# Adding the causal mask on VectorE instead of TensorE, with the values' products moved ahead of the turning of the weights

## The reference

```python
def step(carry, qkv):
    M, z = carry
    q, k, v = qkv
    sq = _sigma(q)                                  # elu(q) + 1
    denom_q = jnp.sum(sq * z[:, :, None, :], axis=-1, keepdims=True) + EPS
    A_mem = jnp.matmul(sq, M) / denom_q
    scores = jnp.matmul(q, jnp.swapaxes(k, -2, -1)) * inv_sqrt_dk
    scores = jnp.where(causal, -jnp.inf, scores)    # above the diagonal of 64 x 64
    A_dot = jnp.matmul(jax.nn.softmax(scores, axis=-1), v)
    A_s = beta * A_mem + (1.0 - beta) * A_dot
    sk = _sigma(k)
    denom_k = jnp.sum(sk * z[:, :, None, :], axis=-1, keepdims=True) + EPS
    V_prev = jnp.matmul(sk, M) / denom_k
    M_new = M + jnp.einsum('bhtk,bhtv->bhkv', sk, v - V_prev)
    z_new = z + jnp.sum(sk, axis=-2)
    return ((M_new, z_new), A_s)
```

## Time and profile before

| what | us |
|---|---|
| median of 3 runs (lowest, highest) | 1970.64 (1970.03, 1977.45) |
| the profiled execution, its own time | 1964.26 |
| its span, first to last instruction | 1962.4 |
| attention stage in it | about 41 to 1268 |
| one pass with look-ahead / with choice | 38.38 / 38.52 |
| busy in the whole span: TensorE, VectorE, ScalarE | 1860.4, 1440.1, 873.7 |

### The profile page before, as it was taken

The page is one execution under the profiler, slowest core; times in us unless marked ns, Lnnn a source line. Parts: engine busy times, 40 slices in busy tenths (PEclk is TensorE's granted clock), DMA queues, the critical chain, the costliest instruction groups (busy, mean ns, idle before and its releaser), DMA issues. The chain is left out here.

```text
span 1962.4 us, 72363 instructions
## 1 busy us (share of the span) xinstructions
PE 1860.4 (95%) x32380; PEld 1575.6 (80%) x32380; DVE 1440.1 (73%) x3478; ACT 873.7 (45%) x1494; POOL 151.6 (8%) x179
## 2 busy tenths in 40 slices
PE   6999999999999999999999999769899999889998
PEld 5888888888888888888888888647776767667997
DVE  7888788888888777777777777566587887876222
ACT  4344344434344443443343434225587777764110
POOL 1000000000000000000000000141100000001000
PEclk9999999999999999999999999779999999999999
DMA  4112111211221121111111112046500000014000
GB/s 146 46 46 78 57 46 49 81 52 46 63 67 41 35 57 46 36 39 59 41 35 44 54 41 67 30 146 184 164 13 12 12 12 22 5 42 161 23 12 22
DMA packets 65668, 109.52 MB, mean 56 GB/s; under 512 B 4736, under 2 KB 25232, under 8 KB 65360
## 3 DMA queue, kind: packets, MB, share of 16 engines
q1 hardware_dynamic: 59584, 85.74, 13.9%
q0 software_dynamic: 5776, 19.15, 3.1%
HBM read 60.31 MB, written 27.26 MB: 45 GB/s over the span
## 5 line engine op out<-in xcount | busy, mean ns | idle before, releaser
L1021 PE MATMUL proj<-xnT_high,held 128*128 128x256 f32 x1536 | 233.8, 287 | 2.1 <-DVE xnT_low L749 2.1
L1021 PEld LDWEIGHTS proj<-xnT_high,held 128*128 128x128 f32 x1536 | 202.5, 190 | 7.8 <-DVE xnT_low L749 2.6
L425 POOL TENSOR_TENSOR As<-T 128x512 f32<-128x512 f32 x64 | 84.4, 1319 | 1173.0 <-DVE T L844 1173.0
L1021 PE MATMUL proj<-xnT_low,held 128*128 128x256 f32 x1024 | 162.9, 281 | 0.0
L2017 DVE CUSTOM_DVE_ANT_0 Sm<-Sp,held 128x1023 f32<-128x1023 f32 x128 | 155.5, 1216 | 9.7 <-DVE r L1278 3.0
L1915 ACT ACTIVATE Sm<-Sm,least 128x1023 f32<-128x1023 f32 x128 | 146.7, 1146 | 13.7 <-DVE least L2017 12.9
L1021 PEld LDWEIGHTS proj<-xnT_low,held 128*128 128x128 f32 x1024 | 139.3, 189 | 0.0
L2063 PE MATMUL Sp<-KS,held 128*128 128x512 f32 x256 | 95.0, 454 | 34.5 <-DVE least L2017 29.4
L484 ACT ACTIVATE Pq<-Pq 128x1024 f32<-128x1024 f32 x64 | 68.0, 1062 | 121.3 <-DVE Pq L813 120.9
L464 ACT ACTIVATE QT<-proj 128x512 f32<-128x512 f32 x64 | 38.0, 594 | 179.9 <-PE proj L1021 179.9
L1967 DVE COPY PTs<-Tp 128x512 f32<-128x512 f32 x128 | 88.1, 688 | 40.3 <-PE Tp L2075 39.9
(11 more groups left out here) (322 smaller groups left out, 4394.1 us busy)
## 6 DMA issues: line engine op xcount, KB each, us to landing
VS<-DV SPq DMA_DIRECT2D x64, 264.0 KB, 3.9
xin<-in_x SPq DMA_DIRECT2D x32, 512.0 KB, 4.9
out_rows<-xu SPq DMA_DIRECT2D x64, 256.0 KB, 2.0
mask_columns<-x1T SPq DMA_DIRECT2D x16, 512.0 KB, 5.4
xs<-in_w SPq DMA_DIRECT2D x16, 512.0 KB, 4.3
xe<-in_x SPq DMA_DIRECT2D x15, 512.0 KB, 3.6
QT<-in_wqT SPq DMA_DIRECT2D x1, 1024.0 KB, 6.2
KT<-in_wkT SPq DMA_DIRECT2D x1, 1024.0 KB, 9.3
```

The costliest lines, as they stand in the source:

```text
L425: pool.tensor_tensor(As[:, :], T1[:, :], T2[:, :], ALU.add).then_inc(s_as, 1)
L1021: ins = pe.matmul(bank[:, g * BT:g * BT + BT], w[hw][:, c, o:o + P], xnT[hx][:, c, :], start=n + c == 0, stop=n == 2 and c == G - 1)
```

## The change

TensorE's four mask products go away, and the scores are written with `start=True`; the wait for `s_t2` moves to the first score product. VectorE, in `row_max`, now first adds `causal` to the scores in four instructions (one for each of the four banks, 128 x 256 each), which read PSUM and write `Pq` in SBUF; the maximum and `less_max` then read `Pq`. On TensorE V0 stands in front of the turning 1, V1 in front of `pv` 1, and SK0, SK1 and XT0 all in front of `memory` 1. ScalarE copies V0 out before the turned weights. Nothing else moves, on any engine.

```diff
@@ ScalarE, half @@
                     feature(m, 1, "KT", KT, pn, 1.0, (s_sq, m * 2 + 4))
+                if stage1:
+                    v_tile(m, pn, 0)
                 p_turned(m, 1)
                 if stage1:
-                    v_tile(m, pn, 0)
                     v_tile(m, pn, 1)
@@ VectorE @@
             def row_max(m, a):
                 dve.wait_ge(s_S, m * 2 + (a + 1))
-                link(dve.tensor_reduce(mx[:, :, :], s_half(a), AX.X, ALU.max))
+                rows = Pq[:, :, :, :].rearrange("p g j k -> p j g k")
+                for j in range(J):
+                    ins = dve.tensor_tensor(rows[:, j, :, :], s_half(a)[:, j, :, :], bm(causal[:, :], G), ALU.add)
+                    if j < J - 1:
+                        done[0] += 1
+                        ins.then_inc(s_dve, 1)
+                link(ins)
+                link(dve.tensor_reduce(mx[:, :, :], rows, AX.X, ALU.max))
 
             def less_max(m, a):
-                dve.tensor_tensor(Pq[:, :, :, :].rearrange("p g j k -> p j g k"), s_half(a),
+                rows = Pq[:, :, :, :].rearrange("p g j k -> p j g k")
+                dve.tensor_tensor(rows, rows,
                                   mx[:, :, :].rearrange("p j (g o) -> p j g o", o=1).broadcast_to([P, J, G, SEG]),
                                   ALU.subtract).then_inc(s_sub, 1)
@@ TensorE @@
-            def mask(m, a):
-
-                pe.wait_ge(s_t2, m * 2 + a + 1)
-                for j in (0, 2, 1, 3):
-                    r = slice((j // 2) * SEG, (j // 2) * SEG + SEG)
-                    pe.matmul(S[:, j, a * 256:a * 256 + 256].rearrange("p (g k) -> p g k", g=G), identb[r, :],
-                              causal[r, :].rearrange("p (o k) -> p o k", o=1).broadcast_to([SEG, G, SEG]),
-                              start=True, stop=False, skip_group_check=True)
-
-            def scores(p, a, b):
+            def scores(m, p, a, b):
+                if b == 0:
+                    pe.wait_ge(s_t2, m * 2 + a + 1)
...
                         ins = pe.matmul(S[b * SEG:b * SEG + SEG, j, o:o + SEG], QT[q, p, g, t:t + SEG],
-                                        KT[q, p, g, t:t + SEG], start=False, stop=(g == G - 1),
-                                        skip_group_check=True)
+                                        KT[q, p, g, t:t + SEG], start=True, stop=True)
@@ TensorE, half @@
-                mask(m, 1)
-                scores(p, 1, 0)
-                scores(p, 1, 1)
+                scores(m, p, 1, 0)
+                scores(m, p, 1, 1)
                 a_and_b(m, p, 1)
                 as_transposes(m, m * 2, 0)
                 if stage1:
                     feature(m, "KT", wk, 1)
-                p_transposes(m, 1)
                 if stage1:
                     values(m, 0)
+                p_transposes(m, 1)
                 t_times_m(m, 2)
+                if stage1:
+                    values(m, 1)
                 pv(m, mh, p, 1)
                 if stage1:
-                    values(m, 1)
-                if stage1:
                     sk_rows(m, n2, 0)
-                memory(m, p, 1)
-                if stage1:
                     sk_rows(m, n2, 1)
                 if ln:
                     x_transposes(m, m + 2, p, "XT", 0)
+                memory(m, p, 1)
                 t_times_m(m, 3)
                 if stage1:
                     denominators(m, n, pn)
-                    mask(m + 1, 0)
-                    scores(pn, 0, 0)
-                    scores(pn, 0, 1)
+                    scores(m + 1, pn, 0, 0)
+                    scores(m + 1, pn, 0, 1)
                     den_transposes(m)
```

More of the change, by code:

```diff
@@ L1255, in _ @@
             x_transposes(None, 1, 1, "XT", 0)
-            mask(0, 0)
-            scores(0, 0, 0)
+            scores(0, 0, 0, 0)
             x_transposes(None, 1, 1, "XT", 1)
-            scores(0, 0, 1)
+            scores(0, 0, 0, 1)
             half(0, 0, 0, first=True)
```

## The result

The changed kernel takes 2108.89 us (median of 4 runs, 2103.41 to 2112.72); before took 1970.99 beside it. The ratio is 1.0686, with a 95% interval of 1.0667 to 1.0706: slower by 138 us. The profiled execution took 2108.63 us, its span 2106.9. The forecast was 2091 in a range of 2045 to 2115.

The account below looks back on a forecast made before the run. TensorE's products bound the kernel now; after the change, waits on VectorE would add 4.1 us to look-ahead passes (62) and 3.7 to choice passes (55), plus 3.5: +120 on 1970.6, so 2091. Own range 2070 to 2115, with rival 1 2045 to 2115.

Parts of the forecast that it names:

- The loop through VectorE: One pass, `a_and_b` 0 to the next, taking the later of TensorE and VectorE: 42.5 us with look-ahead, 42.2 with choice.
- the passes with choice: Passes without router rows, 15 to 29: 42.2 us each against 38.52, +3.7 a pass, 55 us in all.
- The clock: Rival 4: waits halve TensorE's clock from `a_and_b` 0 to `memory` 0; 2364, or 2182 in a third of passes; chance 0.07.
- a clock that leaves 1.00 in mid-stage: One of the signs named in advance that would show the forecast to be wrong.
- The additions: Four of 128 x 256 on VectorE before the maximum: 1.49 us a set, ends 1.13 and 1.73.
- V0's wait, XT0's and the scores' waits: TensorE waiting for `low_a`'s bank at V0 1.1 us, `xn` at XT0 1.4, `memory_part` 1 at scores 0 1.0.
- the time before `a_and_b` 0: TensorE waiting there 1.2 us for L799, `previous_values`, on VectorE.
- The saving of 0.64 us a pass: Two masks of 0.32 us taken off TensorE in each pass; 20.5 us for all 64.
- `start=True` at nothing: Overwriting scores costed at no gain; up to 0.4 us a pass was thought possible.
- Rival 2: TensorE's count decides and VectorE's 6.0 us idle takes the additions: 20.5 us saved, 1950; chance 0.08.
- Rival 3: Waits and savings cancel, within 0.5% (10 us); chance 0.03.
- Rival 1: Fewer waits, V0 does not wait: 1.1 us a pass or 33 us off, 2058; chance 0.12.

Follow-up runs that it names:

- adds_twice: The changed kernel with VectorE's four additions done twice, the second set writing the same values again; 2243.58 us, ratio 1.1381 to the kernel before.
- mask_only: The kernel before with the mask added on VectorE and scores with `start=True`, old TensorE and ScalarE orders kept; 2042.51 us, ratio 1.0360.
- tile_0: The kernel before with VectorE's additions for tile 0 alone, tile 1 keeping its mask products, old order; 2001.06 us, ratio 1.0173.
- tile_1: The kernel before with VectorE's additions for tile 1 alone, tile 0 keeping its mask products, old order; 2002.16 us, ratio 1.0174.
- v0_only: Against mask_only, V0 moved in front of the turning 1 on TensorE and ScalarE; 2047.55 us, ratio 1.0413 to the kernel before.
- low_a_mid: The changed kernel with `low_a` of AST0 between the additions and the maximum of tile 1; 2080.50 us, ratio 1.0564 to the kernel before.
- v1_back: The changed kernel with V1 behind `pv` 1 again, V0 still in front of the turning; 2108.11 us, ratio 1.0702 to the kernel before.

## Why the prediction was right

**The loop through VectorE: right.** Step by step, a look-ahead pass in the rows above against my sum:

| step | forecast, us | measured, us |
|---|---|---|
| `a_and_b` 0 to `memory` 0 | 9.09 | 529.32 - 520.24 = 9.08 |
| to `memory_part` 0, to the additions | 1.00 + 4.75 | 1.00 + 4.75 |
| additions | 1.49 | 1.44 |
| to the end of `low_a` AST0 | 2.39 + 0.68 | 3.08 |
| hand-over, V0 to `pv` 1 | 0.1 + 7.14 | 0.06 + 7.25 |
| `pv` 1 to `softmax_part` 1 | 1.21 | 548.11 - 546.90 = 1.21 |
| to `memory_part` 1 and its end | 5.45 | 510.50 - 505.03 = 5.47 |
| from there to `denominators` | 0.1 + 1.0 + 0.48 = 1.58 | 512.61 - 510.50 = 2.11 |
| to the end of `previous_values` | 6.04 + 1.49 | 518.81 + 1.28 - 512.61 = 7.48 |
| hand-over | 0.1 | 0.15 |

The forecast was 42.5, the pass takes 43.07. With choice 42.2 was forecast and 42.15 measured, and there too step by step: from `a_and_b` 0 at 953.06 it is 19.39 us to V0, 7.24 to `pv` 1, 1.20 to `softmax_part` 1, 5.15 to the end of `memory_part` 1 behind XT0 and `memory` 1, 1.53 to `denominators`, which there does wait for TensorE, and 7.64 to the next `a_and_b` 0.

**Where the 18 us between 2091 and 2109 are.** First, 0.53 us in each look-ahead pass, 8 us in all. This is the one step at which I took the wrong side as the later one: I had TensorE's way over the scores 0 and `den_transposes`, 1.58 us, but VectorE's own queue from the end of `memory_part` 1 to `denominators` takes 2.11. The passes have 43.07 us whether their scores 0 take 0.99 us from start to start (at 122.59), 1.15 as here, or 1.33 (at 165.65). The queue is so long because the router's sum (L617) takes 1.24 us beside GpSimd's addition of T1 and T2, which begins when `memory_part` ends:

```profile
510.63 1.27 POOL L425 TENSOR_TENSOR As<-T 128x512 f32<-128x512 f32 x1 [20.75 <-DVE T L853]
```

The same instruction away from it takes 0.69 (at 508.36 us). No run isolates this, but the fourteen traces show it: each look-ahead pass has one such instruction away from GpSimd's addition, always of 0.69, and one that meets it, and that one ends 0.54 to 0.56 us after the addition whatever the overlap: 0.89 us long where they share 0.35 (most passes of the kernel before), 1.12 where they share 0.57, 1.24 where they share 0.70 (all passes of the changed kernel).

Second, the passes with choice: their usual value came out as said, but the mean of passes 16 to 29 is 43.19, against 38.88 before. That is +4.3 a pass where I had 3.7, 9 us in all. Passes 15 to 29 together lie 16 us above fifteen usual ones; TensorE's stops without a semaphore in them sum up to 9.7 us, and their four stretches at half clock, 13.7 us long, can cost half of that.

**The clock: a rival that was partly there.** I gave 0.07 to waits that cost TensorE its clock, in every or every third pass for 9 us, and I named a clock that leaves 1.00 in mid-stage as a sign of being wrong. That sign came: between 80 and 1380 us of the changed kernel stand five stretches at 0.50, of 3.4 or 6.8 us, where the kernel before had none up to its last pass. They are 20.5 us long, so by half their length, an estimate, they cost about 10 of the 138 us at most. One of them in the timeline:

```profile
812.05 0.50 PE L1077 MATMUL S<-KT,QT 32*64 32x64 f32 x17 [0.65 <-DVE T L853]
814.17 0.82 PE L1077 MATMUL S<-KT,QT 32*64 32x64 f32 x47 [1.62 <-issue]
...
816.11 2.06 PE L1185 MATMUL proj<-wo_high,AT_high 128*128 128x512 f32 x4
```

The scores 0 wait 0.65 us, stop again for 1.62 in the middle of a group with no semaphore behind it ("issue"), and the transposes and the output projection after it run at half speed: the first four products take 2.06 us and not 1.18. The pass has 44.68 us. adds_twice shows such falls in almost every pass. The Trainium skill ("TensorE: Matmul & The Clock Gate", section "HAM oscillation — how this bites in real kernels") has idle gaps between bursts as the cause of such falls; the trace agrees that they come behind waits and stops, and no run here isolates them. Waits alone are not enough: mask_only, with waits of up to 1.6 us, 65 us in all from 100 to 1200 us, has no stretch at 0.50 from 80 us to its last pass, nor have tile_0, tile_1 and v0_only. All kernels with TensorE's new order have them, and of the 41 in those other than adds_twice, 32 begin within 3 us of a stop without a semaphore.

**The stops without a semaphore.** They existed before (one of 1.3 us in the earlier trace rows); in the changed kernel they are 8.3 us from 100 to 1200 us. The traces show what ends them. TensorE's instructions come over DMA queue 8 in packets of 16 KB, 255 in the run, and one of them landed at 812.75 us, 1.42 before TensorE went on at 814.17. The DMA view of 811 to 812.8 us has it:

```profile
q8 instruction: 1, 0.02, 3.0%
```

All 91 stops over 0.3 us from 100 to 1200 us in the fourteen traces end 1.2 to 1.7 us after such a packet has landed. With 168 packets in these 1100 us of the changed kernel, one every 6.5 us, one stop in thirteen would do so by chance. So these are waits for instructions, as far as the times can show it. In the changed kernel the packet came 8 to 15 us behind the one before, where the median is 5.2; why it comes late, and so why the choice passes have most of the stops, stays open.

**The additions: right, a little dear.** 1.44 for 1.49, and 415 ns each for 424. Between the two readings that I weighed, overlap by the rows or 1.73 without any, the rows had it. Four of 0.415 in 1.41 us overlap by 0.08 each, as I took; the pair of L799 has 0.69 + 0.69 - 1.28 = 0.10, and not the 0.09 that I wrote. Maximum and subtraction kept their price too (538.91 - 536.51 = 2.40 for 2.39). The Trainium skill's advice in "VectorE: DVE Perf Modes", section "The TRN2 errata — SBUF-src ops pay a fixed extra latency per instruction", to make tiles larger still holds: one instruction for four takes 1215 ns and gave 0.40 us a pass, though the four overlap and their source is PSUM.

**V0's wait, XT0's and the scores' waits: right in place, V0's and XT0's a little smaller than forecast** (forecast 1.1, 1.4 and 1.0; 0.86, 1.2 and 0.96 in the timeline). One wait I placed wrongly: of the time before `a_and_b` 0 the larger part (0.83) is spent at AST1, which needs OUT0's bank from `out_rows`. The end of `previous_values` decides both ways, so the sum does not change. low_a_mid, tile_0, tile_1 and mask_only confirm that these steps follow one another in one loop.

**The saving of 0.64 us a pass: too high**, as a price for the mask on TensorE. By itself it is worth 12 us, not 20.5, since 0.28 us after it the loop through VectorE takes over. This did not touch the forecast, where the loop decides anyway. `start=True` at nothing was right: 64 score products take 1.00 us from start to start (533.52 to 534.52) and took 0.99 (519.31 to 520.30).

**Rival 2, TensorE's count decides,** falls: 6 us of idle time on VectorE in a pass took nothing of the 2.9. **Rival 3**, waits and savings cancel, falls with 138 us. **Rival 1**, V0 without a wait, is what low_a_mid made by an edit: 28 us less than the changed kernel (24 by the ratios), where I had said 33.

## What to carry to other kernels

Where one engine is busy all the time, look for the second loop right below it before moving work from it: walk once round a pass and take at each hand-over the later side, and the slack that is left (here 0.28 us) is all that the other engine can take, whatever its idle share. Moving a product in front of a consumer covers what it stands before, and delays everything that hangs behind that consumer on the other engine; look at what is queued there (here the next rows' normalisation and `memory_part`, for which the next scores wait).

## What the runs showed of the hardware beyond the expected

- TensorE stopped in the middle of a group of products, up to 2.6 us and without a semaphore, until 1.2 to 1.7 us after its next 16 KB of instructions had landed: once from 100 to 1200 us in the kernel before, 14 times in v1_back. An edit of the order alone changed how often.
- Stretches of 3.4 or 6.8 us at the 1.2 GHz level in mid-stage came with waits of TensorE together with such stops: five in the changed kernel, none in the kernel before up to its last pass, and none in mask_only with its 65 us of waits. In adds_twice, with waits of up to 2.4 us, most look-ahead passes have one (1.6 us a pass), and 30 of its 36 stand beside no stop. A cost that grows in small steps thus grew by a jump: 135 us where the additions alone were 89.
- The same VectorE instruction (L617, 128x512, two inputs in SBUF) took 0.69 us at one place of the pass and 1.24 at another, beside GpSimd's addition, and ended 0.54 to 0.56 us after it in every pass in which the two met.
